# The upper halves of the attention one-hots made by ScalarE between its table copies

## The chip, the cores and the metric

The kernel runs on one core of one Trainium2 chip, as one launch. The metric is the device time of the launch in microseconds; the median of three runs of the kernel before is 3207.38 us (3206.33 to 3209.21). TensorE does the matrix products (PE in the rows, PEld for its weight loads), VectorE is DVE, ScalarE is ACT, GpSimd is POOL and SyncE, which issues most DMAs, is SP.

## The reference

Four graph layers run one after the other on 3750 nodes with 256 features, each on the layer-normalised, relu'd input, each added to it. The graph has 63750 edges, sorted by destination, with a type of 8 each. The change touches the first layer, a graph attention with one weight per edge type:

```python
feat_all = jnp.einsum('ni,rhid->rnhd', inputs, conv_weights)
feat_src_e = feat_all[edge_type, edge_src]
feat_dst_e = feat_all[edge_type, edge_dst]
el = jnp.sum(feat_src_e * attn_l[edge_type], axis=-1)
er = jnp.sum(feat_dst_e * attn_r[edge_type], axis=-1)
e = jax.nn.leaky_relu(el + er, negative_slope=LEAKY_SLOPE)
m = jax.ops.segment_max(e, edge_dst, num_segments=N_NODES)
ex = jnp.exp(e - m[edge_dst])
denom = jax.ops.segment_sum(ex, edge_dst, num_segments=N_NODES)
alpha = ex / denom[edge_dst]
h = jax.ops.segment_sum(alpha[..., None] * feat_src_e, edge_dst, num_segments=N_NODES)
```

The three layers behind it (a graph convolution, a network with edge features and a mean aggregation) are left as they are.

## The kernel before

Nodes lie in 30 tiles of 128, edges in 500 tiles of 128 that are gathered, weighted and summed by one-hot products. Each engine has its own program, written out in order; semaphores with the names below tie them together. Ahead of the loop over the edge tiles stands a prologue with three jobs that run side by side:

- **The table.** For each of the 30 node tiles TensorE computes the features of all 8 types in four parts (`table_part`, L871), two products of 128x512 each, into the PSUM banks 4 to 7 in turn. ScalarE copies each part (L599), before the four of a tile the attention terms of the sources (L595), and then writes the tile to HBM as `feat_d` (L603). A part waits for the copy of the part four before it (`tab_free`).
- **The attention term of the destinations, er.** For the 500 edge tiles, 50 iterations of ten, in two halves of five. SyncE loads the edges' places, counted from a node tile's start, into every partition (`RB`, from `rel_d`, L339). VectorE compares them with 0 to 127 (L1410, "low") and 128 to 255 (L1411, "high"), since five neighbouring edge tiles can reach over two node tiles; `OHT` holds both. TensorE multiplies them with er per node (`er_half`, L881 for low, L882 for high). VectorE reduces the result (L1430), multiplies it with the edge types (L1437) and sums it (L1440). At the start of each iteration TensorE's sequencer loads ten offsets into registers (L894).
- **Counts of equal edges.** VectorE counts them for four tiles an iteration (L1417) and writes them as bf16 (L1424, `val_ready`); GpSimd scatters them into the adjacency matrix `a_d` in HBM (L523). The first 200 tiles are done in the prologue.

On TensorE a half is put behind the table part at which its share of the 120 parts is reached: 100 halves to 120 parts. VectorE's order in an iteration is reduction of a half, both one-hots of the same half of the iteration after it, the same for the second half, product, sum, counts. The one-hots' buffer has one place for each half (0 and 1), so a half's one-hots wait for TensorE's half two before. Behind the loop GpSimd waits for its scatters, for VectorE and for all of `feat_d` in HBM, and gathers the 500 edge tiles (L532) among the remaining scatters.

Of the kernel before, what the change touches and what calls it, by code (L numbers as in the profile page):

```python
# [17 lines left out]
ALU = mybir.AluOpType  # L18
ACT = mybir.ActivationFunctionType
# [27 lines left out]
def gnn(nc, x, src, dst, edge_attr, edge_type, conv_w, attn_l, attn_r, h_bias, gcn_w, gcn_b, cluster,  # L47
# [10 lines left out]
    NT = -(-N // P)  # L58
# [5 lines left out]
    IT = T // 10  # L64
# [24 lines left out]
    with ExitStack() as ctx:  # L89
# [22 lines left out]
        IOTP = sb("IOTP", [P, 2])  # L112
# [42 lines left out]
        OHT = HSF[:, 4000:5280].bitcast(BF16).rearrange("p (h q e) -> p h q e", h=2, q=2)  # L155
# [33 lines left out]
        RB = [v.bitcast(BF16).rearrange("p (h e) -> p h e", h=2) for v in (SA[:, 6144:6784], SA[:, 7296:7936])]  # L189
# [67 lines left out]
        def s(name):  # L257
            if name not in S:
                S[name] = sem(name)
            return S[name]  # L260
# [36 lines left out]
        def mine(eng, ins, name, value):  # L297

            ins.then_inc(s(name), 1)
            eng.wait_ge(s(name), value)  # L300
# [16 lines left out]
        def counted_at(n):  # L317
# [3 lines left out]
            new = (k + 1) * CB // NB > k * CB // NB  # L321
            return c if new and c < T else None

        def ring(t):

            return SL[:, t % 10, :]
# [10 lines left out]
        def _(sp):  # L337
            def load(dst_ap, src_ap, name):
                sp.dma_start(dst_ap, src_ap).then_inc(s(name), 16)  # L339
# [6 lines left out]
            for a, t in ((dst, DI), (src, SI), (edge_type, TI)):  # L346
                v = t.rearrange("t (b e) -> t b e", b=LB)
                load(v[:, 0:LB - 1, :], a[0:(LB - 1) * LT * P].rearrange("(b t e) -> t b e", b=LB - 1, e=P), "edges_in")
                n = EFULL - (LB - 1) * LT
# [40 lines left out]
            with sp.Fori(0, IT // 2) as w:  # L390
                for b in range(2):
                    u = 2 * w + b
                    for h in range(2):
                        sp.wait_ge(s("oht_ready"), 2 * u + h + 1)
                        load(RB[b][:, h, :], rel_d[bass.ds((10 * u + 5 * h) * P, 5 * P)].partition_broadcast(P),
                             f"rows{b}_in{h}")
                    sp.wait_ge(s("val_ready"), u + 1)
                    load(KEYR[:, b, :, :].rearrange("p k n -> p (k n)"),
                         key_d[bass.ds(CT * u * P, CT * P)].partition_broadcast(P), f"rows{b}_in1")
# [167 lines left out]
        def _(act):  # L567
# [19 lines left out]
            act.wait_ge(s("small_in"), 16 * 15)  # L587
            act.activation(B1C, B1C, ACT.Relu).then_inc(s("b1_relu"), 1)

            act.wait_ge(s("elr_done"), 2 * 4)  # L590
            for t in range(NT):
                i = t % 2
                if t >= 2:
                    act.wait_ge(s(f"stage_out{i}"), 16 * (t // 2))
                act.activation(STAGE[:, i, :, D:RW], ELS[:, t, :].rearrange("p (r h) -> p r h", r=R),  # L595
                               ACT.Copy).then_inc(s("tab_el"), 1)
                for q in range(4):
                    act.wait_ge(s("tab_ps"), 4 * t + q + 1)
                    act.activation(STAGE[:, i, 2 * q:2 * q + 2, 0:D], PS[:, 4 + q, :].rearrange("p (r n) -> p r n", r=2),  # L599
                                   ACT.Copy).then_inc(s("tab_free"), 1)  # L600
                act.wait_ge(s("tab_free"), 4 * t + 8)
                act.wait_ge(s("tab_el"), t + 1)
                act.dma_start(rows(feat_d, t), STAGE[:, i, :, :].rearrange("p r n -> p (r n)")).then_inc(s(f"stage_out{i}"), 16)  # L603

            for i in range(2):
                act.wait_ge(s(f"stage_out{i}"), 16 * NJ)
            act.wait_ge(s("cont_ready"), 1)
# [212 lines left out]
        def _(pe):  # L820
# [53 lines left out]

            def er_half(u, h, qs):
                pe.wait_ge(s("oht_ready"), 2 * u + h + 5)
                pe.wait_ge(s("er_done"), 2 * u + h + 1)
                for k in range(5):
                    o = PS[:, h, k * 3 * RH:(k + 1) * 3 * RH]
                    q = qs[5 * h + k]  # L880
                    pe.matmul(o, OHT[:, h, 0, k * P:(k + 1) * P], ERB[:, bass.ds(q, 3 * RH)], start=True, stop=False)  # L881
                    last = pe.matmul(o, OHT[:, h, 1, k * P:(k + 1) * P], ERB[:, bass.ds(q + 3 * RH, 3 * RH)],  # L882
                                     start=False, stop=True)
                last.then_inc(s("er_ps"), 1)
# [3 lines left out]
            halves = 0  # L888
            for n in range(4 * NT):
                table_part(n // 4, n % 4)  # L890
                if halves * 4 * NT <= n * 2 * IT:
                    u, h = halves // 2, halves % 2
                    if h == 0:
                        _, qs = nc.values_load_multi_w_load_instructions(  # L894
                            QR[:, 10 * u:10 * u + 10], engines=[PE], min_val=0, max_val=(NT - 1) * 3 * RH,
                            skip_runtime_bounds_check_because="clamped to the last node tile when it was computed")
                    er_half(u, h, qs)
                    halves += 1
# [373 lines left out]
        def _(dve):  # L1272
# [134 lines left out]
            def dst_one_hot(u, h, b, v):  # L1407

                dve.wait_ge(s(f"rows{b}_in{h}"), 16 * (1 + h) * (v + 1))
                ts(OHT[:, h, 0, :], RB[b][:, h, :], IOTP[:, 0:1], None, ALU.is_equal)  # L1410
                mine(dve, ts(OHT[:, h, 1, :], RB[b][:, h, :], IOTP[:, 1:2], None, ALU.is_equal), "oht_ready", 2 * u + h + 5)  # L1411

            def counts(u, b):

# [537 lines left out]
```

## Time and profile before

| | |
|---|---|
| median of the runs | 3207.38 us |
| profiled execution, whole time | 3211.49 us |
| profiled execution, span of the program | 3209.7 us |
| TensorE busy | 2858.9 us (89%) |
| VectorE busy | 1866.8 us (58%) |
| ScalarE busy | 1257.0 us (39%) |
| GpSimd busy | 1017.9 us (32%) |
| first table part | 118.92 us |
| first gather of edge tiles | 478.57 us |

Times in the rows are microseconds from the span's start, unless marked ns. A timeline row gives the start, the duration, the engine, the line, the operation and, in brackets, the time that the engine stood idle before it and what ended that. The name there is the latest of the instructions that set a semaphore for it.

### The profile page before, as it was taken

The page shows a single profiled execution, that of the slowest core. Times are in us where ns is not written, and L with a number is a line of the kernel's source. Part 1 is how long each engine was busy: PE and PEld are TensorE (multiplying, and loading weights), DVE is VectorE, ACT ScalarE, POOL GpSimd, SP SyncE. Part 2 cuts the span into 40 slices and gives each one's busy share as a digit, 9 for nine tenths or more (in the row PEclk, how much of TensorE's full clock was granted, in tenths as well). Part 3 has the DMA queues.
Part 4 walks back from the last instruction along what each step waited for, and adds up shares of the span by engine and source line. Part 5 has one row for each costly group of instructions (what it writes and reads, how often), then busy time and mean ns, then how long its engine had stood idle before and what let it go on. Part 6 is the DMA issues. An engine that isn't in the chain of part 4 may idle for free.

```text
span 3209.7 us, 48246 instructions
## 1 busy us (share of the span) xinstructions
PE 2858.9 (89%) x15034; PEld 1892.2 (59%) x15034; DVE 1866.8 (58%) x5317; ACT 1257.0 (39%) x3665; POOL 1017.9 (32%) x1048
## 2 busy tenths in 40 slices
PE   1789885999999989897788999799999999999998
PEld 1544444999899888887144444455555555545446
DVE  6578884888878766667235433355555555513334
ACT  1122225787778777774004000144444444401000
POOL 3065567777777777776000000000000000000000
PEclk6599986999999999996968999899999999999999
DMA  8966654333333333321843333300000000132232
GB/s 237 402 187 183 194 173 112 101 91 89 89 86 88 89 86 87 88 55 34 299 146 118 102 102 100 106 7 3 7 5 5 7 3 7 38 102 70 83 102 78
DMA packets 245030, 317.60 MB, mean 99 GB/s; under 512 B 121467, under 2 KB 162084, under 8 KB 240740
## 3 DMA queue, kind: packets, MB, share of 16 engines
q1 hardware_dynamic: 191412, 179.07, 19.7%
q0 software_dynamic: 49104, 104.11, 10.9%
q10 hardware_dynamic: 4320, 31.95, 2.5%
q8 instruction: 108, 1.77, 0.2%
q14 instruction: 86, 0.70, 0.1%
HBM read 237.42 MB, written 77.59 MB: 98 GB/s over the span
## 4 chain that ended last, share of the span: by engine, by line
PE 49%; DVE 23%; issue 9%; ACT 5%; POOL 5%; DMA 5%; DVEq 4%; SPq 0%; POOLq 0%
PE PS L1153 17%; PE PS L998 15%; DVE SUMS L1567 4%; DMA BG<-a_d 3%; PE PS L822 3%; PE PS L939 3%; POOL BG L532 3%; PE PS L964 3%; PE PS L977 3%; POOL a_d L523 2%; ACT BG L653 2%; DVE BG L1703 2%; DVEq L1582 2%; DVE OHB L1430 2%; DVE X L1573 1%
## 5 line engine op out<-in xcount | busy, mean ns | idle before, releaser
L523 POOL DMA_INDIRECT a_d<-VAL,IDXS x499 | 492.4, 987 | 241.4 <-issue 135.9
L1153 PE MATMUL PS<-BG,SL 128*128 128x512 f32 (+1 forms) x1440 | 534.7, 527 | 12.2 <-ACT SL L736 12.2
L532 POOL DMA_INDIRECT BG<-feat_d,IDXST x500 | 490.4, 981 | 152.5 <-issue 127.2
L653 ACT ACTIVATE BG<-BG,SL 128x64 f32<-128x64 f32 x2000 | 513.5, 337 | 0.0
L1567 DVE TENSOR_TENSOR SUMS<-SUMS,PS 128x640 f32 x500 | 409.0, 818 | 165.6 <-PE PS L939 153.4
L1153 PEld LDWEIGHTS PS<-BG,SL 128*128 128x128 f32 x1440 | 273.9, 193 | 250.6 <-issue 222.4
L564 POOL MEMSET BG<- 128x7680 f32 x1 | 6.5, 6499 | 1297.1 <-DVE MV L1834 1297.1
L939 PE MATMUL PS<-OHB,BG 128*128 128x128 f32 x2000 | 339.2, 293 | 0.0
L977 PE MATMUL PS<-OHB,X 128*128 128x128 f32 x2000 | 319.5, 283 | 1.7 <-DVEq L1545 1.7
L977 PEld LDWEIGHTS PS<-OHB,X 128*128 128x128 f32 x2000 | 289.7, 197 | 14.7 <-issue 1.7
L964 PE MATMUL PS<-W1A,X 65*128 65x256 f32 x1000 | 276.0, 399 | 3.9 <-ACT X L627 0.9
L939 PEld LDWEIGHTS PS<-OHB,BG 128*128 128x128 f32 x2000 | 271.0, 197 | 0.6
L871 PE MATMUL PS<-SUMS,BG 128*128 128x512 f32 x480 | 244.1, 640 | 0.0
L723 ACT ACTIVATE SM<-SM,EPSC 128x1 f32<-128x1 f32 x60 | 17.7, 295 | 543.4 <-DVE SM L1795 543.4
L634 ACT ACTIVATE X<-PS 128x512 f32<-128x512 f32 x250 | 148.9, 596 | 154.9 <-PE PS L964 154.3
L822 PE MATMUL PS<-IDENT,X 128*128 128x128 f32 (+3 forms) x650 | 148.3, 274 | 65.9 <-DVE X L1486 26.8
L998 PE MATMUL PS<-AL,BG 128*128 128x512 bf16 (+1 forms) x924 | 193.2, 368 | 4.0 <-ACT BG L702 2.6
L998 PE MATMUL PS<-AL,SUMS 128*128 128x512 bf16 (+1 forms) x912 | 189.0, 364 | 3.9 <-DVE X L1906 2.8
L964 PEld LDWEIGHTS PS<-W1A,X 65*128 65x128 f32 x1000 | 175.4, 195 | 28.7 <-ACT X L627 8.5
L736 ACT ACTIVATE SL<-PS,COL 128x128 f32<-128x128 f32 x480 | 174.1, 476 | 26.0 <-PE PS L822 25.9
L599 ACT ACTIVATE SUMS<-PS 128x512 f32<-128x512 f32 x120 | 71.7, 597 | 272.5 <-PE PS L871 272.5
L1703 DVE TENSOR_TENSOR SUMS<-SUMS,OHB 128x2 f32 x499 | 81.6, 164 | 159.5 <-issue 93.5
(298 smaller groups left out, 4084.2 us busy)
## 6 DMA issues: line engine op xcount, KB each, us to landing
BG<-a_d SPq DMA_DIRECT2D x171, 256.0 KB, 4.2
AL<-a_d SPq DMA_DIRECT2D x137, 256.0 KB, 2.6
a_d<-BG POOLq DMA_DIRECT2D x30, 1088.0 KB, 40.4
feat_d<-SUMS ACTq DMA_DIRECT2D x30, 1040.0 KB, 5.0
BG<-rel_d SPq DMA_DIRECT2D x100, 160.0 KB
X<-in_edge_attr_dram SPq DMA_DIRECT2D x124, 128.0 KB
SUMS<-a_d SPq DMA_DIRECT2D x52, 256.0 KB, 2.6
SL<-key_d SPq DMA_DIRECT2D x50, 256.0 KB
```

The costliest lines, as they stand in the source:

```text
L523: pool.indirect_dma_start(a_d.rearrange("n (w o) -> (n w) o", o=1), bass.IndirectOffsetOnAxis(ap=IDXS[:, t:t + 1], axis=0), VAL[:, t:t + 1 ...
L532: pool.indirect_dma_start(RING[:, t // NB % 3, t % NB, :], None, feat_d.rearrange("n (r d) -> (n r) d", r=R), bass.IndirectOffsetOnAxis(ap ...
L653: last = act.activation(m, m, ACT.Copy, scale=EXT[:, b % 2, k, 1 + q:2 + q])
L736: last = act.activation(H1T[:, i, c, :], PS[:, 4 + 2 * i + c // 4, (c % 4) * P:(c % 4 + 1) * P], ACT.Relu, scale=COL8[:, 2 * l, c:c + 1], ...
L822: return pe.transpose(out_ap, in_ap, IDENT[0:k, 0:k])
L871: last = pe.matmul(PS[:, 4 + q, :], HT[:, c, t * P:(t + 1) * P], WALL[:, c, q * 512:(q + 1) * 512], start=(c == 0), stop=(c == 1))
L939: last = pe.matmul(at[:, (c + 1) * P:(c + 2) * P], RING[:, b % 3, k, c * P:(c + 1) * P], OH[:, k % 10, :], start=True, stop=True)
L964: last = pe.matmul(EDGE_HIDDEN[:, k * D:(k + 1) * D], EAT[v % 2][:, 2 * q + k, :], W1A[:, :], start=True, stop=True)
L977: pe.matmul(SUM_AT[n % 3][:, (3 + c) * P:(4 + c) * P], HM[v % 2][:, k, c * P:(c + 1) * P], OH[:, n % 10, :], start=True, stop=True)
L998: last = pe.matmul(PS[:, 4 * (g % 2) + 2 * c + o // 512, 0:m], lhs(t, part)[:, c * P:(c + 1) * P], rhs[:, o:o + m], start=(t == 0 and part ...
L1153: last = pe.matmul(PS[:, to + q, 0:width], lhs[:, i, c, :], w[:, c, q * width:(q + 1) * width], start=(c == 0), stop=(c == kc - 1))
L1567: add = tt(a, a, SUM_AT[n % 3].rearrange("p (a n) -> p a n", a=5), ALU.add)
```

## The change

The high one-hot leaves VectorE. ScalarE makes it with two operations: the absolute difference of the edges' places and 128 to 255, and the relu of one minus that, which is 1 where the difference is 0 and 0 elsewhere. Two pairs stand ahead of the table's copies; then, after the copy of a part behind which TensorE has a half, the pair for the half that comes two later. A new semaphore `oht_high` tells of it: TensorE waits for it before a half and SyncE before it loads a row buffer again. The rule by which halves stand among the parts is written as a function that both engines use; it gives TensorE the same order as before.

```diff
+        def halves_before(n):
+            return min(2 * IT, (n - 1) * 2 * IT // (4 * NT) + 1) if n else 0
...
                         sp.wait_ge(s("oht_ready"), 2 * u + h + 1)
+                        sp.wait_ge(s("oht_high"), 2 * u + h + 1)
                         load(RB[b][:, h, :], rel_d[bass.ds((10 * u + 5 * h) * P, 5 * P)].partition_broadcast(P),
...
+            def high_one_hot(u, h):
+                b, v = u % 2, u // 2
+                act.wait_ge(s(f"rows{b}_in{h}"), 16 * (1 + h) * (v + 1))
+                if u >= 1:
+                    act.wait_ge(s("er_ps"), 2 * (u - 1) + h + 1)
+                step(act.activation(OHT[:, h, 1, :], RB[b][:, h, :], ACT.Abs, bias=IOTP[:, 1:2], scale=-1.0))
+                act.activation(OHT[:, h, 1, :], OHT[:, h, 1, :], ACT.Relu, bias=1.0, scale=-1.0).then_inc(s("oht_high"), 1)
+
+            act.sem_inc(s("oht_high"), 4)
+            for h in range(2):
+                high_one_hot(0, h)
+            highs = 2
             act.wait_ge(s("elr_done"), 2 * 4)
...
+                    if highs < 2 * IT and halves_before(4 * t + q + 1) > highs - 2:
+                        high_one_hot(highs // 2, highs % 2)
+                        highs += 1
...
                 pe.wait_ge(s("oht_ready"), 2 * u + h + 5)
+                pe.wait_ge(s("oht_high"), 2 * u + h + 5)
...
-                if halves * 4 * NT <= n * 2 * IT:
+                if halves < halves_before(n + 1):
...
-                ts(OHT[:, h, 0, :], RB[b][:, h, :], IOTP[:, 0:1], None, ALU.is_equal)
-                mine(dve, ts(OHT[:, h, 1, :], RB[b][:, h, :], IOTP[:, 1:2], None, ALU.is_equal), "oht_ready", 2 * u + h + 5)
+                mine(dve, ts(OHT[:, h, 0, :], RB[b][:, h, :], IOTP[:, 0:1], None, ALU.is_equal), "oht_ready", 2 * u + h + 5)
```

ScalarE at the start of the table, before (the tile SUMS holds several buffers by name, the staging of the table among them; BG holds the row buffers; x20 is a count):

```order
L578 ACTIVATE SL<-X,NBI,RS 128x256 [waits n0_tp] x20
L588 ACTIVATE COL<-COL 128x2 [waits small_in]
L595 ACTIVATE SUMS<-SUMS 128x8x4 [waits elr_done]
L599 ACTIVATE SUMS<-PS 128x2x256 [waits tab_ps] x4
L603 DMA feat_d<-SUMS 128x2080 [waits tab_el,tab_free]
```

The same place after:

```order
L593 ACTIVATE COL<-COL 128x2 [waits small_in]
L601 ACTIVATE SUMS<-BG,IOTP 128x640 [waits rows0_in0]
L602 ACTIVATE SUMS<-SUMS 128x640 [waits act_steps]
L601 ACTIVATE SUMS<-BG,IOTP 128x640 [waits rows0_in1]
L602 ACTIVATE SUMS<-SUMS 128x640 [waits act_steps]
L613 ACTIVATE SUMS<-SUMS 128x8x4 [waits elr_done]
L617 ACTIVATE SUMS<-PS 128x2x256 [waits tab_ps]
L601 ACTIVATE SUMS<-BG,IOTP 128x640 [waits er_ps,rows1_in0]
L602 ACTIVATE SUMS<-SUMS 128x640 [waits act_steps]
L617 ACTIVATE SUMS<-PS 128x2x256 [waits tab_ps] x2
```

The absolute differences (L601) and relus (L602) now stand between the copies (L617), two pairs of them ahead of the first, and a copy waits behind the rows and the half that its pair waits for.

VectorE at the start of an iteration in its loop, before:

```order
L1430 TENSOR_REDUCE OHB<-PS 128x160 [waits er_ps]
L300 REGISTER_ALU
L1409 ISA [waits er_done]
L1410 TENSOR_SCALAR SUMS<-BG,IOTP 128x640 [waits rows1_in0]
L1411 TENSOR_SCALAR SUMS<-BG,IOTP 128x640
L300 ISA
L1429 REGISTER_ALU [waits oht_ready]
```

The same place after:

```order
L1452 TENSOR_REDUCE OHB<-PS 128x160 [waits er_ps]
L300 REGISTER_ALU
L1432 ISA [waits er_done]
L1433 TENSOR_SCALAR SUMS<-BG,IOTP 128x640 [waits rows1_in0]
L300 ISA
L1451 REGISTER_ALU [waits oht_ready]
```

One of the two one-hots is gone; every wait of VectorE stands as before.

## Rows read from the trace of the kernel before

**Rows 1.** Sums by engine: stretch, length, busy (count); granted clock, DMA share, GB/s.

```profile
169.30:472.88 303.58, 276.81 (x1364) 138.89 (x1365) 243.78 (x782) 71.89 (x137) 179.60 (x185) 0.96 0.62 183
```

**Rows 2.** Groups of instructions, 169.3 to 472.88: count | busy, mean ns | idle before.

```profile
L599 ACT ACTIVATE SUMS<-PS 128x512 f32<-128x512 f32 x110 | 65.7, 597 | 224.8 <-PE PS L871 224.8
...
L1410 DVE TENSOR_SCALAR SUMS<-BG,IOTP 128x640 bf16<-128x640 bf16 x92 | 40.9, 445 | 12.4
L1411 DVE TENSOR_SCALAR SUMS<-BG,IOTP 128x640 bf16<-128x640 bf16 x92 | 34.8, 378 | 0.0
...
L595 ACT ACTIVATE SUMS<-SUMS 128x32 f32<-128x32 f32 x27 | 6.2, 229 | 11.3 <-ACT SUMS L599 11.3
```

**Rows 3.** Timeline of one iteration, 302 to 306 us, VectorE and one half.

```profile
303.69 0.37 DVE L1411 TENSOR_SCALAR SUMS<-BG,IOTP 128x640 bf16<-128x640 bf16 x1
...
304.20 0.21 PE L881 MATMUL PS<-BG,SUMS 128*128 x1 [1.17 <-DVE SUMS L1411]
...
304.97 0.39 DVE L1410 TENSOR_SCALAR SUMS<-BG,IOTP 128x640 bf16<-128x640 bf16 x1
...
305.28 0.38 DVE L1411 TENSOR_SCALAR SUMS<-BG,IOTP 128x640 bf16<-128x640 bf16 x1
...
305.84 0.49 DVE L1437 TENSOR_TENSOR OHB<-OHB,SUMS 128x320 f32<-128x320 f32 x1 [0.19 <-DVE SUMS L1411]
```

**Rows 4.** Waits in 169.3 to 472.88: engine and releaser, total us, times, longest.

```profile
PE PS L881 <- DVE SUMS L1411: 24.6, 21, 1.8
PE PS L881 <- DVE OHB L1430: 1.7, 2, 1.1
...
DVE OHB L1430 <- PE PS L882: 8.7, 4, 5.1
```

**Rows 5.** TensorE's register loads, ns min/median/max: all 50, and that near 307.

```profile
L894 PEldq TENSOR_LOAD <-BG x50: 1072/2412/10539, 117.0 to 466.2; - x50
...
L894 PEldq TENSOR_LOAD <-BG x1: 3911/3911/3911, 307.1 to 307.1; - x1
```

**Rows 6.** Timeline of TensorE, 307 to 318 us.

```profile
307.19 0.21 PE L881 MATMUL PS<-BG,SUMS 128*128 x1
...
307.61 1.95 PE L871 MATMUL PS<-SUMS,BG 128*128 128x512 f32 x4
311.25 0.21 PE L881 MATMUL PS<-BG,SUMS 128*128 x1 [1.69 <-DVE SUMS L1411]
...
312.52 5.00 PE L871 MATMUL PS<-SUMS,BG 128*128 128x512 f32 x8
```

**Rows 7.** ScalarE's groups by form over the whole span: count | busy, mean ns.

```profile
L653 ACT ACTIVATE BG<-BG,SL 128x64 f32<-128x64 f32 x2000 | 513.5, 337 | 0.0
...
L765 ACT ACTIVATE SUMS<-SL 128x512 f32 x39 | 25.0, 641 | 23.7 <-DVE SL L1857 12.6 <-DVE SL L1851 11.1
...
L702 ACT ACTIVATE BG<-SL 128x1280 bf16<-128x1280 f32 x6 | 7.6, 1270 | 0.2
```

**Rows 8.** Timeline of the start: first copy, second low one-hot, a late half.

```profile
122.74 0.60 ACT L599 ACTIVATE SUMS<-PS 128x512 f32<-128x512 f32 x1 [11.93 <-PE PS L871]
...
134.90 0.39 DVE L1410 TENSOR_SCALAR SUMS<-BG,IOTP 128x640 bf16<-128x640 bf16 x1 [2.61 <-DMA SL<-key_d]
...
148.05 0.26 PE L881 MATMUL PS<-BG,SUMS 128*128 x1 [6.49 <-issue]
```

**Rows 9.** Timeline of the prologue's end: last values, scatter, table write, first gather.

```profile
472.81 0.17 DVE L1424 CAST VAL<-BG 128x4 bf16<-128x4 f32 x1
...
473.25 0.95 POOL L523 DMA_INDIRECT a_d<-VAL,IDXS  x1 [0.84 <-DVE VAL L1424]
...
473.73 0.33 ACTq L603 DMA_DIRECT2D feat_d<-SUMS  x1
...
478.57 0.99 POOL L532 DMA_INDIRECT BG<-feat_d,IDXST  x1 [0.44 <-issue]
...
508.33 0.29 DVE L1484 TENSOR_TENSOR X<-BG,AL 128x80 f32<-128x80 f32 x1 [19.37 <-DMA BG<-feat_d,IDXST]
```

More of the change, by code:

```diff
@@ L603, in _ @@
                 act.dma_start(rows(feat_d, t), STAGE[:, i, :, :].rearrange("p r n -> p (r n)")).then_inc(s(f"stage_out{i}"), 16)
+            assert highs == 2 * IT
             for i in range(2):
```

## Prediction
> **What bounds the kernel now.** I first looked where the two engines that the change touches work together: the prologue, in which TensorE alternates table parts with halves of the attention term, VectorE makes the one-hots and counts, and ScalarE only copies. I took it as the stretch from 169.30 us (the reduction of iteration 3, after the DMA crowd of the start) to 472.88 us (that of iteration 49): 46 iterations in 303.58 us, 6.60 us each. In the sums by engine [rows 1] TensorE is busy 276.81 us, VectorE 243.78, ScalarE 71.89. A share of 80% does not make VectorE look like the limit, so the next view is the order of its work [rows 3]: reduction of a half, one-hot low, one-hot high, the same for the second half, product, sum, counts. Between these operations stand only short gaps in which it waits for its own result (0.19 us before the product at 305.84). The waits say the same [rows 4]: VectorE waited 8.7 us for TensorE in the whole stretch, four times, one of them 5.1 us at its very beginning. VectorE therefore sets the pace, by a chain of its own work.
>
> TensorE is close behind. It waited 24.6 us for the one-hots by the profile [rows 4]. That is too much, because a second thing holds the first half of an iteration: TensorE's sequencer loads ten offsets from SBUF into registers, 1.07 to 10.54 us, median 2.41 [rows 5]. The half at 311.25 is put down to the one-hot, but the load that began at 307.1 took 3.91 us and ended at 311.0 [rows 5, 6]. The half at 304.20 is a true wait for VectorE: the one-hot high of that half ended at 304.06 [rows 3]. A half released that late takes 1.27 us to the next table part (311.25 to 312.52), and one that was ready 0.42 us (307.19 to 307.61) [rows 6].
>
> **VectorE loses one operation per half.** The first one-hot runs from 304.97 to 305.36, the second, which starts before the first is done, from 305.28 to 305.66 [rows 3]; without it the chain goes on from 305.36. That is 0.30 us per half, not the 0.378 us of the operation [rows 2], because the two overlap. With 92 halves in the stretch it makes 27.6 us; VectorE alone would then need 276.0 us, 6.00 us per iteration. The iterations before 169.30 us I count at nothing: there the register load holds TensorE, 6.49 us before the half at 148.05 [rows 8], and a shorter VectorE chain only waits longer.
>
> **ScalarE gains 200 operations.** No row shows this shape; the nearest ones are 128x512 in 641 ns and 128x1280 in 1270 ns, both SBUF to SBUF [rows 7]. The line through them gives 0.82 ns a column and 746 ns for 640. The first of the pair has a bias by partition; a 128x64 with one such operand takes 337 ns [rows 7], 63 above that line, so 0.81 us. The relu follows only when the absolute difference is written. The bounds of that wait are 0 and 0.42 us (11.3 us in 27 waits of ScalarE for itself, each with a DMA issue in it [rows 2]); I take 0.1, since the issue fills most of the 0.42. The pair costs 1.66 us (1.56 to 1.98). An iteration has two pairs, 110/46 = 2.4 copies of 0.597 us [rows 2] and 0.6 of the 0.23 us copies with their 0.42 us wait: 3.3 + 1.4 + 0.4 = 5.1 us (4.9 to 5.8), under the 6.0 us of VectorE. ScalarE idles 224.8 us for table parts in the stretch [rows 2]; 92 pairs take 153 us of it. Price of the position: a pair stands ahead of the next copy, and waits for the half two before its own. TensorE has four banks for parts, so a copy that is one pair (1.7 us) late holds nothing, and the pair has two halves and two parts of time before it is needed (2 x (0.42 + 1.95) us, of which the pair takes 1.7) [rows 6]. I put it at zero; without this cover each iteration would pay up to 1.7 us. The Trainium skill speaks against the change: "ScalarE: Activation LUTs", Rules for kernel authors, wants relu and the like on VectorE, up to about three times faster per element in bf16. The trace agrees on the operation (0.378 us against my 1.66). The same page, What ACT_TABLE_LOAD costs, would price the pair at 719 + 812 = 1.53 us, an estimate by its formula, and the iteration at 4.9 us.
>
> **Waits that are added.** SyncE waits for the high one-hot too before it refills a row buffer; queued behind are the other row loads and the key loads. The high half needs only TensorE's half two before it, the low one VectorE's reduction of that half too, so the new wait is met first: zero (if it came last, a row load would go out later by up to the 1.7 us of a pair, and it has an iteration of time). At the start two pairs stand ahead of all table copies, and the second needs the rows and keys on which VectorE waited until 134.90 us; the first copy goes from 122.74 to about 137 us [rows 8]. Four free banks hide it: part 4 is the first that needs a bank back, and it stands behind the half at 148.05 us. Uncovered it would cost 14 us. TensorE checks one more semaphore per half: between 0 and 0.14 us, which is all that passes from the end of a one-hot to the half that it releases (304.06 to 304.20) [rows 3]. While TensorE is not the limit this is zero; if it were, 92 halves would pay at most 13 us.
>
> **What is late next.** TensorE. Its stretch without true waits lies between two bounds. If half of the 26.3 us of waits [rows 4] was the register load and everything else stays, it needs 303.6 - 13 = 290 us. If all waits go, and with them the 0.85 us by which each of the 23 late halves was slow, it needs 303.6 - 26.3 - 19.6 = 258 us. Some table parts also run slow after such a wait: two took 5.00 us at 312.52 instead of 1.95 each [rows 6], at a mean granted clock of 0.96 of the 2.4 GHz level in the stretch [rows 1]. The result is the later of 276 (VectorE) and 258 to 290 (TensorE), with some waiting of each for the other. I take the middle of 276 and 290, 283 us: a gain of 20.6. At the end the table's last write is issued at 473.73 and the first gather starts at 478.57, right after the last four scatters, which follow from the values written at 472.81 [rows 9]. If TensorE now trails VectorE, that write comes later by part of a microsecond: -0.6. From the gather the chain runs on (VectorE waits 19.37 us for the first twenty, until 508.33), so the prologue's gain moves all behind it.
>
> Sum: 3211.49 - 20.6 + 0.6 = 3191.5 us in the profiled execution, which lies 4.1 above the median of 3207.38; as a median 3187.4 us.
>
> **The rivals.**
> - TensorE keeps the pace. The register load gets longer when the row and key loads come closer together, and holds the first half of each iteration. For it: 3.91 us at 307.1 against a minimum of 1.07, and 10.54 when the DMA queues were full [rows 5]. Against it: in half of the waits VectorE was last. The stretch is 290 to 300 us; gain 3 to 13, 3194 to 3204.
> - The wait only changes its name, or a later stage gives the gain back. Halves would wait for the high one-hot instead of the low, if a pair took about 2.3 us (two pairs 4.6, with 1.8 of copies 6.4). Nothing before 508 us is tied to a fixed time, which speaks against the second form. 3201 to 3213.
> - ScalarE takes over and it is slower. This is the page's rule as a mechanism of this kernel: work goes to the engine that is slower at it. The place is the pair between two copies, and it decides from (6.60 - 1.8)/2 = 2.4 us per pair. At 2.7 us an iteration takes 7.2, 0.6 more than now, 28 us in 46: 3235 us. The rows of 641 and 1270 ns [rows 7] speak against it.
>
> **How the numbers follow.** Forecast (stretch 276 to 290, 3179 to 3194): 0.64. TensorE keeps the pace: 0.15. No change: 0.10. ScalarE: 0.07. More than VectorE's 27.6 us (slow table parts vanish too): 0.04. This measurement can tell about 0.2%, 6.4 us, from no change, so faster means below 3201. Faster: 0.64 + 0.11 + 0.04 = 0.79. Same: 0.04 + 0.10 = 0.14. Slower: 0.07. The range reaches from a little beyond VectorE's whole gain, 3178, to the end of the first rival, 3203.
>
> **What would show it.** In the changed kernel VectorE's iteration should be 6.0 to 6.3 us, its waits for TensorE's halves should grow from the 8.7 us, and TensorE's waits for the low one-hot should fall below 24.6. The pair on ScalarE should take 1.6 to 2.0 us and no half should wait for the high one-hot. The first gather should start at 455 to 465 us instead of 478.57. I am wrong if the pair is above 2.3 us, if register loads of 4 us become common, or if the first gather comes earlier and the end does not.

## The result and the profile after

The changed kernel takes 3187.25 us (median of 5 runs, 3185.04 to 3194.47) against 3208.3 us (5 runs) for the kernel before beside it: a ratio of 0.9933 with a 95% interval of 0.9914 to 0.9951. That is 21 us faster, at the predicted time of 3187.4. The profiled execution took 3186.24 us, its span 3184.4 us. The nearness to the predicted median hides that some terms were off and cancelled, so the trace is read first.

The same stretch, reduction of iteration 3 to that of iteration 49, now runs from 170.85 to 449.33 us. Its sums by engine in the changed kernel (stretch, length; busy us and count of PE, PEld, DVE, ACT, POOL; granted clock, DMA share, GB/s) answer to [rows 1]:

```profile
170.85:449.33 278.48, 264.04 (x1362) 133.46 (x1363) 217.00 (x690) 206.56 (x321) 174.25 (x182) 0.98 0.67 199
```

The stretch went from 303.57 to 278.48 us, 6.60 to 6.05 per iteration. VectorE has 92 instructions fewer and is busy 26.8 us less, 0.29 per half; ScalarE has 184 more and 134.7 us more.

The groups by form of the stretch (count | busy, mean ns of one | idle before, releasers) answer to [rows 2]:

```profile
L601 ACT ACTIVATE SUMS<-BG,IOTP 128x640 bf16<-128x640 bf16 x92 | 75.7, 822 | 42.8 <-PE PS L905 41.5 <-DMA SL<-key_d 1.3
L602 ACT ACTIVATE SUMS<-SUMS 128x640 bf16<-128x640 bf16 x92 | 67.8, 737 | 2.9
L617 ACT ACTIVATE SUMS<-PS 128x512 f32<-128x512 f32 x110 | 65.6, 597 | 28.6 <-PE PS L893 20.1
...
L1433 DVE TENSOR_SCALAR SUMS<-BG,IOTP 128x640 bf16<-128x640 bf16 x92 | 41.0, 446 | 12.4
```

The pair is 0.822 + 0.737 us and a gap of 0.03, 1.59 us. ScalarE idled 224.8 us for table parts before; now it still idles 42.8 and 28.6 us, in front of pairs and copies. One low one-hot costs VectorE what it did (446 ns against 445).

The timeline of VectorE in one iteration (start, length, engine, line, operation) answers to [rows 3]. L1452 is the reduction, L1433 the low one-hot, L1459 the product:

```profile
304.96 0.66 DVE L1452 TENSOR_REDUCE OHB<-PS 128x160 f32<-128x480 f32 x1
...
305.76 0.62 DVE L1433 TENSOR_SCALAR SUMS<-BG,IOTP 128x640 bf16<-128x640 bf16 x1
...
306.51 0.66 DVE L1452 TENSOR_REDUCE OHB<-PS 128x160 f32<-128x480 f32 x1
...
307.29 0.39 DVE L1433 TENSOR_SCALAR SUMS<-BG,IOTP 128x640 bf16<-128x640 bf16 x1
...
307.87 0.49 DVE L1459 TENSOR_TENSOR OHB<-OHB,SUMS 128x320 f32<-128x320 f32 x1 [0.19 <-DVE SUMS L1433]
```

The product waits for the one remaining one-hot by the same 0.19 us by which it waited for the second one before. VectorE's chain is still without a long gap, one link shorter.

The waits of the stretch (releaser: total us, times, longest) answer to [rows 4]:

```profile
PE PS L904 <- DVE SUMS L1433: 10.1, 13, 1.8
PE PS L904 <- DVE OHB L1452: 3.4, 3, 1.5
PE PS L904 <- issue: 0.6, 2, 0.3
...
DVE OHB L1452 <- PE PS L905: 11.8, 8, 6.2
```

TensorE's waits for VectorE fell from 26.3 to 13.5 us. Of VectorE's 11.8 us, 6.2 stand ahead of the very first reduction, as 5.1 of the 8.7 did before; inside the stretch it waits 5.6 us for TensorE, 3.6 before. None of the halves in the stretch waits for ScalarE.

These rows name the semaphore that came last and never a register load. So the ends of the loads (L894 before, L917 after) and of the one-hots were compared half by half in the two traces: a wait is the load's where the load ended after the one-hot. Before, 10.2 us (7 halves) were the load's and 16.2 us (16 halves) the one-hot's; after, 9.7 us (9 halves) are the load's and 4.5 us (9 halves) the one-hot's. The waits for the one-hot fell, those for the loads stayed.

At the prologue's end the timeline (with what ended an engine's idle time in brackets) answers to [rows 9]:

```profile
449.25 0.17 DVE L1446 CAST VAL<-BG 128x4 bf16<-128x4 f32 x1
...
449.70 0.96 POOL L528 DMA_INDIRECT a_d<-VAL,IDXS  x1 [0.86 <-DVE VAL L1446]
...
451.08 0.33 ACTq L624 DMA_DIRECT2D feat_d<-SUMS  x1
...
455.84 0.99 POOL L537 DMA_INDIRECT BG<-feat_d,IDXST  x1 [1.40 <-DMA feat_d<-SUMS]
...
485.61 0.29 DVE L1506 TENSOR_TENSOR X<-BG,AL 128x80 f32<-128x80 f32 x1 [19.38 <-DMA BG<-feat_d,IDXST]
```

The first gather starts 22.73 us earlier (455.84 against 478.57), and VectorE's wait for the first twenty gathers is 19.38 us against 19.37. The account: 25.1 gained in the stretch, 1.54 lost ahead of it, 0.82 lost behind it, where the first gather now waits for the table's last write, and idles 1.40 us instead of 0.44. From the gather to the end it is 2728.6 us against 2731.1.

### The profile page after: what moved, and what is told of

Same layout as the page of the kernel before. It is cut to its first block, busy times and chain, and to the rows that moved or that the text cites. A ratio compares the mean times of both kernels' runs of the same rounds, so it can differ in the third digit from the quotient of the medians.

```text
span 3184.4 us, 48481 instructions
## 1 busy us (share of the span) xinstructions
PE 2844.6 (89%) x14970; PEld 1887.5 (59%) x15034; DVE 1838.6 (58%) x5217; ACT 1403.1 (44%) x3865; POOL 1015.7 (32%) x1048
## 4 chain that ended last, share of the span: by engine, by line
PE 51%; DVE 23%; issue 8%; ACT 6%; DMA 5%; POOL 4%; DVEq 4%; SPq 0%; POOLq 0%
PE PS L1176 17%; PE PS L1021 15%; DVE SUMS L1589 4%; DMA BG<-a_d 3%; PE PS L987 3%; PE PS L844 3%; PE PS L962 3%; PE PS L1000 3%; ACT BG L675 3%; DVE BG L1725 2%; POOL BG L537 2%; DVEq L1604 2%; POOL a_d L528 2%; DVE OHB L1452 2%; DVE X L1595 2%
## 5 line engine op out<-in xcount | busy, mean ns | idle before, releaser
L528 POOL DMA_INDIRECT a_d<-VAL,IDXS x499 | 488.8, 980 | 219.4 <-issue 134.7
L987 PE MATMUL PS<-W1A,X 65*128 65x256 f32 x1000 | 276.0, 399 | 3.9 <-ACT X L649 0.9
L745 ACT ACTIVATE SM<-SM,EPSC 128x1 f32<-128x1 f32 x60 | 17.7, 295 | 540.7 <-DVE SM L1817 540.7
L893 PE MATMUL PS<-SUMS,BG 128*128 128x512 f32 x480 | 240.0, 631 | 0.0
L1725 DVE TENSOR_TENSOR BG<-BG,OHB 128x2 f32 x499 | 81.9, 164 | 144.7 <-issue 85.8
```

The costliest lines, as they stand in the source:

```text
L528: pool.indirect_dma_start(a_d.rearrange("n (w o) -> (n w) o", o=1), bass.IndirectOffsetOnAxis(ap=IDXS[:, t:t + 1], axis=0), VAL[:, t:t + 1 ...
L893: last = pe.matmul(PS[:, 4 + q, :], HT[:, c, t * P:(t + 1) * P], WALL[:, c, q * 512:(q + 1) * 512], start=(c == 0), stop=(c == 1))
L987: last = pe.matmul(EDGE_HIDDEN[:, k * D:(k + 1) * D], EAT[v % 2][:, 2 * q + k, :], W1A[:, :], start=True, stop=True)
L1725: step(tt(a, a, held[:, :, n:n + 1], ALU.add))
```

## The experiments

**The theory:** VectorE's chain set the pace, so the operation taken from it is the whole gain, and ScalarE's pair is hidden by the two halves of lead with which it is issued. **The rivals:** the pair has a price somewhere; TensorE, with its register loads, sets the pace after the change. The part behind the first gather varies between 2725 and 2744 us from one profiled execution to another, so the stretch, reduction 3 to reduction 49, is the sharper measure. Each stretch is that of one profiled execution; two kernels whose stretches should be equal differ by 0.2 us (before and e1) and 1.8 us (after and e2). All ratios are to the kernel before, run beside.

| kernel | stretch us | first gather us | median us | ratio, 95% interval |
|---|---|---|---|---|
| before | 303.57 | 478.57 | 3208.3 | 1 |
| after | 278.48 | 455.84 | 3187.25 | 0.9933, 0.9914 to 0.9951 |
| e1, operation back on VectorE | 303.35 | 479.31 | 3207.42 | 1.000, 0.9991 to 1.001 |
| e2, before without the high one-hot | 280.29 | 455.97 | 3191.53 | 0.9947, 0.9931 to 0.9964 |
| e3, half an operation more on ScalarE | 283.90 | 461.44 | 3192.19 | 0.9949, 0.9933 to 0.9966 |
| e4, a whole one more | 288.26 | 466.11 | 3198.41 | 0.9972, 0.9963 to 0.9982 |
| e5, after with one register load | 275.10 | 439.39 | 3172.48 | 0.9876, 0.9855 to 0.9897 |
| e8, before with one register load | 302.54 | 467.52 | 3195.61 | 0.9963, 0.9949 to 0.9977 |
| e6, pair one half ahead | 323.42 | 500.84 | 3234.06 | 1.0074, 1.0058 to 1.0089 |
| e11, e6 with one register load | 275.29 | 441.13 | 3176.93 | 0.99, 0.9881 to 0.9918 |
| e7, after, a load of 20 every second iteration | 273.17 | 449.81 | 3172.63 | 0.9884, 0.9867 to 0.9902 |
| e9, before, the same loads of 20 | 301.13 | 465.57 | 3200.35 | 0.9968, 0.9959 to 0.9978 |
| e10, after, loads of 30 | 316.01 | 493.05 | 3225.02 | 1.0044, 1.0028 to 1.0059 |

### e1 and e2: is it VectorE's operation?

e1 keeps ScalarE's pair and gives VectorE its second one-hot again, written to a place that nobody reads:

```diff
+        SCR = OHB[:, 840:1160].bitcast(BF16)
...
-                mine(dve, ts(OHT[:, h, 0, :], RB[b][:, h, :], IOTP[:, 0:1], None, ALU.is_equal), "oht_ready", 2 * u + h + 5)
+                ts(OHT[:, h, 0, :], RB[b][:, h, :], IOTP[:, 0:1], None, ALU.is_equal)
+                mine(dve, ts(SCR, RB[b][:, h, :], IOTP[:, 1:2], None, ALU.is_equal), "oht_ready", 2 * u + h + 5)
```

> The changed kernel, with VectorE making its second one-hot again, into a place that nobody reads; ScalarE, the waits and TensorE stay as changed. Theory (the gain is VectorE's shorter chain and nothing else): the 46 iterations from the reduction of iteration 3 to that of iteration 49 take 303 us again instead of 278.5, and the time is back at 3208, between 3204 and 3213. Rival (the gain comes from elsewhere, the waits or the released upper half): it stays near 3187.

e2 is the kernel before without the high one-hot: nothing in its place, on either engine; the upper halves are set to zero once, ahead of the loop.

```diff
+            step(dve.memset(OHT[:, :, 1, :], 0.0))
...
-                ts(OHT[:, h, 0, :], RB[b][:, h, :], IOTP[:, 0:1], None, ALU.is_equal)
-                mine(dve, ts(OHT[:, h, 1, :], RB[b][:, h, :], IOTP[:, 1:2], None, ALU.is_equal), "oht_ready", 2 * u + h + 5)
+                mine(dve, ts(OHT[:, h, 0, :], RB[b][:, h, :], IOTP[:, 0:1], None, ALU.is_equal), "oht_ready", 2 * u + h + 5)
```

> The kernel before without the high one-hot: it is zero all through, so the part of er that lies in a second node tile is left out; ScalarE does only its copies. Theory (ScalarE's 200 operations and their waits cost nothing): as the changed kernel, 3187 within 4 us, stretch 276 to 280 us. Rival (the pairs hold something that the profile does not show): 3180 or less.

The sums by engine of the stretch, e1 first, then e2 (columns as above):

```profile
170.04:473.39 303.35, 276.82 (x1364) 138.74 (x1365) 244.23 (x782) 207.93 (x321) 176.52 (x183) 0.96 0.59 183
```

```profile
169.13:449.42 280.29, 266.37 (x1362) 133.95 (x1363) 216.90 (x690) 72.00 (x137) 176.26 (x184) 0.97 0.64 198
```

e1 has the ScalarE of the changed kernel (207.93 us) and the VectorE of the kernel before (244.23 us), and the stretch of the kernel before, to 0.2 us. e2 has the VectorE of the changed kernel and the ScalarE of the kernel before, and the changed kernel's stretch within 1.8 us. So the whole gain is VectorE's operation. ScalarE's pair costs nothing that can be seen: without it the stretch is no shorter.

### e3 and e4: what a pair may cost

Both add a copy of the one-hot onto itself behind the relu, of 320 columns (e3) and of 640 (e4), so that the pair becomes longer and its result later. The edit of e4:

```diff
-                act.activation(OHT[:, h, 1, :], OHT[:, h, 1, :], ACT.Relu, bias=1.0, scale=-1.0).then_inc(s("oht_high"), 1)
+                step(act.activation(OHT[:, h, 1, :], OHT[:, h, 1, :], ACT.Relu, bias=1.0, scale=-1.0))
+                act.activation(OHT[:, h, 1, 0:640], OHT[:, h, 1, 0:640], ACT.Copy).then_inc(s("oht_high"), 1)
```

> The changed kernel with a third ScalarE operation in each pair, a copy of 320 columns onto itself: the pair goes from 1.59 to about 2.07 us, ScalarE's iteration from 5.0 to about 5.9 us, just under the 6.05 of the changed kernel. Theory (ScalarE has an iteration's remainder as its slack): 3187 to 3192. Rival (ScalarE is already near its limit, because it waits in order for TensorE): 46 x 0.96 us slower, up to 3231.

> As the run before, but with all 640 columns copied: the pair takes about 2.36 us, ScalarE's iteration about 6.5 us. Theory (ScalarE then sets the pace): the stretch grows by 46 x 0.45 = 21 us to about 300 us, 3208, so that the whole gain is gone. Rival (the two halves of lead hide it): 3187 to 3192.

ScalarE's groups in the stretch of e4 (L601, L603 and L618 are the absolute difference, the added copy and the table copy):

```profile
L601 ACT ACTIVATE SUMS<-BG,IOTP 128x640 bf16<-128x640 bf16 x92 | 75.4, 820 | 18.1 <-PE PS L906 18.0
...
L603 ACT ACTIVATE SUMS<-SUMS 128x640 bf16<-128x640 bf16 x92 | 67.8, 737 | 2.9
...
L618 ACT ACTIVATE SUMS<-PS 128x512 f32<-128x512 f32 x110 | 63.6, 582 | 4.1 <-PE PS L894 3.9
```

In e4 a pair takes 2.36 us, ScalarE is busy 262.0 of 288.3 us and idles 26 us, 0.6 in an iteration of 6.27; half of the stretch's gain is still there in time (288.3 lies 15.3 below 303.6 and 9.8 above 278.5). In e3 a pair takes about 2.07 us and the stretch is 5.4 us longer than the changed kernel's, though the intervals of the whole times overlap. The price in the stretch thus begins between 1.6 and 2.1 us a pair, before ScalarE is full. In e4 VectorE waits 22.2 us for TensorE's halves, in the changed kernel 11.8; without the waits ahead of the first reduction that is 17.7 against 5.6, which covers the 9.8. TensorE's waits for halves there, 23 us before 19 halves, were each ended by a register load that finished after the pair's result: a late pair seems to push back the next load, as is shown for e6 below. e3 came out at the edge of what was expected (3187 to 3192), e4 between its two expectations. By the working of the prediction's third rival, an iteration with e4's pair takes 2 x 2.36 + 1.8 = 6.5 us, hardly less than before; it takes 6.27. That working thus puts the end of the gain too early, and it says nothing of its beginning to shrink: at 2.36 us 10 of the 25 us are gone.

### e6 and e11: what the lead of two halves is worth

e6 issues each pair one half ahead of its use instead of two:

```diff
-                    if highs < 2 * IT and halves_before(4 * t + q + 1) > highs - 2:
+                    if highs < 2 * IT and halves_before(4 * t + q + 1) > highs - 1:
```

> The changed kernel with each pair on ScalarE one half later, so that it is made one half before it is needed instead of two. Theory (the lead of two halves is the cover of the pair): a ready half comes 0.42 + 1.95 us after the half before it, copy and pair take 0.6 + 1.6 us behind the part, so the pair is ready at about the moment of need; halves wait for the high one-hot now and then, TensorE trails, stretch 279 to 290 us, 3187 to 3199. Rival (the lead is not needed): stretch 278.5 within 1 us, 3187. Rival (a late pair holds every half): 300 us or more.

The stretch grew to 323.42 us, 44.9 more than the changed kernel's, and the kernel is slower than before the change. From the timelines of e6, first the relu of one half on ScalarE, then TensorE's halves (L904) and table parts (L893):

```profile
279.31 0.74 ACT L602 ACTIVATE SUMS<-SUMS 128x640 bf16<-128x640 bf16 x1
```

```profile
280.24 0.21 PE L904 MATMUL PS<-BG,SUMS 128*128 x1
...
281.55 1.95 PE L893 MATMUL PS<-SUMS,BG 128*128 128x512 f32 x4
284.26 0.21 PE L904 MATMUL PS<-BG,SUMS 128*128 x1 [0.77 <-issue]
...
285.52 1.95 PE L893 MATMUL PS<-SUMS,BG 128*128 128x512 f32 x4
287.30 0.21 PE L904 MATMUL PS<-BG,SUMS 128*128 x1
```

TensorE idled only 0.1 us before the half at 280.24: the relu had ended at 280.05, while a table part was still running. But the half took 1.31 us to the next part (281.55), where one that had been released long before takes 0.42 (307.56 to 307.98 in the changed kernel). The expectation (279 to 290 us) failed, and no row of these halves shows a long wait for the relu. The rows of TensorE's sequencer in e6 tell what lies between its products, and what comes after the half (count: ns min/median/max, first and last start):

```profile
L904 PEldq FUSED_REGOPS  x500: 46/46/46, 132.7 to 494.9; - x167
```

```profile
L917 PEldq TENSOR_LOAD <-BG x1: 2413/2413/2413, 281.5 to 281.5; - x1
```

Each product of a half has an address operation of 46 ns on the sequencer (500 on L904, as many on L905). In these timelines the operations of a half start 124 ns apart, with one longer step, and the two halves differ in when they start. First those of the low products in the changed kernel's half at 307.56, then those in e6's half at 280.24:

```profile
L904 PEldq FUSED_REGOPS  x5: 46/46/46, 306.4 to 307.4; - x5
```

```profile
L904 PEldq FUSED_REGOPS  x5: 46/46/46, 280.1 to 281.3; - x5
```

In the changed kernel they began 1.1 us ahead of the half, while TensorE worked off a table part, and its products then started 42 ns apart. In e6 the first began at 280.14, behind the relu's end at 280.05, and the products came 124 ns apart, at the pace of the operations. The register load of the next iteration starts only behind the late half, at 281.5, takes 2.41 us, and the next half at 284.26 comes late and slow again (1.26 us). Counting the halves of the last 47 iterations whose ten products take over 0.7 us gives 54 of 94 in e6, 41 before, 29 in the changed kernel. Against the changed kernel e6's halves take about 20 us more in the stretch. Register loads that end after the relu and the one-hot hold 19 halves for 27.7 us, 18 us more, and the table parts take 6 us more, at a granted clock of 0.96 instead of 0.98. These are sums over TensorE's work in the two traces; the waits for the one-hot, which fell, go against them.

If that is the reason, the lead is worth nothing once loads and address operations are gone. e11 is e6 with the load of iteration 0 for all iterations, which also takes the address operations away:

```diff
-                    if h == 0:
+                    if h == 0 and u == 0:
```

> Pairs one half later and one register load for all iterations (er from the wrong node tiles), in which TensorE also has no address operations between the products of a half after the first iteration. Theory (the pairs one half later cost 45 us because a half that is released late takes 1.25 instead of 0.42 us, its address operations not being done ahead): without them the stretch is 276 to 285 us, 3172 to 3182. Rival (the late pair holds TensorE by itself): the stretch stays above 300 us, 3215 or more.

Sequencer and stretch of e11:

```profile
L904 PEldq FUSED_REGOPS  x10: 46/46/46, 132.9 to 138.3; - x10
```

```profile
160.18:435.47 275.29, 242.39 (x1359) 116.20 (x1357) 216.08 (x692) 202.11 (x319) 183.09 (x192) 1.00 0.71 211
```

With the pair issued as late as in e6, the stretch is 275.29 us; all of the loss is gone. So the price of a short lead is not the wait itself but what the wait keeps TensorE's sequencer from doing. Loads and address operations went together here; no run at this lead takes away only one of them, and e6's sums above put the two at about the same.

### e5, e8, e7, e9 and e10: the register loads

e5 is the changed kernel and e8 the kernel before, both with the line of e11's diff.

> The changed kernel with one register load instead of 50: TensorE uses the ten offsets of iteration 0 in all iterations, so er is taken from the wrong node tiles. Theory (VectorE sets the pace also after the change, TensorE's loads only lengthen it a little, from 6.00 to 6.05 us): the stretch from iteration 3 to 49 goes from 278.5 to 276 us, and the two late halves of the start (loads of 10 us) go, some 8 to 10 us: 3176. Rival (TensorE with its loads now sets the pace): the stretch falls to 265 us or less, 3165 or less.

> The kernel before with one register load instead of 50, the offsets of iteration 0 throughout, er from the wrong node tiles. Theory (VectorE alone set the pace): the stretch from iteration 3 to 49 stays at 301 to 303 us, and only the start gains 8 to 10 us: 3199. Rival (the loads shared in the pace already): stretch below 298 us.

The waits of the stretch in e5, to be held against those of the changed kernel:

```profile
PE PS L904 <- DVE SUMS L1433: 32.3, 27, 1.4
...
DVE SUMS L1433 <- DMA SL<-key_d: 3.2, 2, 1.7
DVE OHB L1452 <- PE PS L905: 0.7, 3, 0.2
```

```profile
311.12 0.22 PE L904 MATMUL PS<-BG,SUMS 128*128 x1 [1.22 <-DVE SUMS L1433]
...
311.56 1.95 PE L893 MATMUL PS<-SUMS,BG 128*128 128x512 f32 x4
```

In e5 VectorE waits 0.7 us for TensorE and TensorE 32.3 us for the low one-hot: VectorE sets the pace. The 275.1 us are not its chain alone, since it waits 3.2 us for key loads, which it does not do in the changed kernel; e7 below, where it waits for neither, takes 273.2. A half that is released late is as fast as any, 0.44 us (311.12 to 311.56). In e8 the stretch is 302.54 us, 1.0 less than before, with 2.3 us of waits for keys in it; before, VectorE had waited 3.6 us for TensorE inside the stretch. **Before the change loads and address operations had little share in the pace**, at most 3.6 of 303.6 us, and more in the start, where the reduction of iteration 3 comes at 159.45 us instead of 169.31.

e7 keeps all offsets but loads 20 at a time, in every second iteration; e9 does that to the kernel before, and e10 loads 30 at a time.

```diff
-                    if h == 0:
+                    if h == 0 and u % 2 == 0:
...
-                            QR[:, 10 * u:10 * u + 10], engines=[PE], ...
+                            QR[:, 10 * u:10 * u + 20], engines=[PE], ...
...
-                    er_half(u, h, qs)
+                    er_half(u, h, qs[10 * (u % 2):])
```

> The changed kernel with one register load of 20 offsets for two iterations instead of one of ten for each, 25 instead of 50. Theory (a load costs mostly by itself and not by its count): iteration 1 finds its offsets loaded, one of the two 10 us stalls of the start goes, 5 us, and the stretch falls by 1 to 2 us: 3181. Rival (a load costs by the offset): the loads take twice as long, the stretch grows, 3187 or more.

> The kernel before with one register load of 20 offsets for two iterations. Theory (VectorE alone paced the kernel before, TensorE's loads only its start): stretch 302 to 303 us, one of the two late halves of the start goes: 3200 to 3204. Rival (fewer loads help whatever paces): 3195 or less, as much as they brought to the changed kernel.

> The changed kernel with one register load of 30 offsets for three iterations, 17 in all. Theory (VectorE paces at 5.95 us with few loads as with one): stretch 272 to 276 us as with 25 loads, the start 5 us earlier than with them since iterations 1 and 2 find their offsets loaded: 3165 to 3173. Rival (a long load holds TensorE as much as two short ones): 3175 or more.

TensorE's register loads in the changed kernel (the answer to [rows 5]), in e7 and in e10:

```profile
L917 PEldq TENSOR_LOAD <-BG x50: 1074/2410/10357, 117.7 to 443.6; - x50
```

```profile
L917 PEldq TENSOR_LOAD <-BG x25: 1356/1387/5027, 129.6 to 432.0; - x25
```

```profile
L917 PEldq TENSOR_LOAD <-BG x17: 1364/7101/20322, 116.4 to 475.2; - x17
```

The sums of e7's stretch (columns as above):

```profile
170.97:444.14 273.17, 260.13 (x1360) 130.95 (x1358) 216.54 (x691) 206.27 (x322) 175.90 (x184) 1.00 0.68 208
```

Twenty offsets take a median of 1.39 us where ten take 2.41, and there are half as many. e7's stretch is 273.2 us, 5.3 below the changed kernel's, more than the 1 to 2 expected: the 5.6 us for which VectorE waited there are gone, and its waits show none for TensorE and none for keys. So 273.2 us is VectorE's own chain. The address operations are all still there, with 27 slow halves against 29, so slow halves alone do not hold VectorE; the loads do. e7's median 3172.63 is the fastest of all kernels here that compute the whole: 14.6 us under the changed kernel. In its profiled execution (3189.3 us) the first load began 12 us later than in the others, at 129.6, so the first gather at 449.81 shows less of the gain than the median does. In e9 the same edit gives 2.4 us in the stretch and about 10 ahead of it, and 9.6 us (0.32%) in all. So most of e7's 14.6 us could have been had before the change too; about 5 are new. Loads of 30 have a median of 7.1 us. TensorE waits for 39.4 us before 7 halves, each behind a load that ends 0.3 us earlier, and e10 is slower than before the change, as its rival had it. Why 30 are so much slower than 20 stays open.

## Why the prediction was right, and where it was not

The bound and the mechanism held: VectorE's chain set the pace, and one link less is the gain. The time held too, its closeness by luck. Point by point:

- **The operation removed: right.** 0.30 us per half was read from starts that overlap, instead of the operation's 0.378; VectorE's busy time fell by 0.29 per half. Its chain alone was put at 276.0 us; where nothing else holds it, it takes 273.2 (e7). The 276.0 still held the 3.6 us for which VectorE had waited inside the stretch; 303.6 - 3.6 - 27.6 gives 272.4.
- **What is late next: mis-sized.** I took 283 us, the middle between VectorE's 276 and a TensorE bound of 290; it was 278.5, a gain of 25.1 instead of 20.6. That half of TensorE's waits were register loads and would stay was not far off: 10.2 of 26.3 us, and 9.7 afterwards. The step that failed is "everything else stays" in the 290. TensorE's time in the halves fell by 6.8 us, with 29 slow halves instead of 41, and that in the table parts by 4.4 us, at a granted clock of 0.98 instead of 0.96. The 278.5 are VectorE's chain of 273.2 (e7) and the 5.6 us for which it waits inside the stretch, to 0.3 us. Taking the middle of two bounds came near it without that working.
- **A half released late is slow: right in size, wrong in cause.** The 0.85 us do not come with the late release by itself: e5's late half takes 0.44 us. They come with address operations that were not done ahead (e6's timelines). I counted 23 such halves, those with a wait; 41 of the last 94 were slow.
- **ScalarE's pair: right.** 1.59 us against 1.66 (1.56 to 1.98). By the formula of the Trainium skill ("ScalarE: Activation LUTs", What ACT_TABLE_LOAD costs) the two operations come to 812 and 719 ns, an estimate; the trace agrees, with 822 and 737. The Trainium skill ("ScalarE: Activation LUTs", Rules for kernel authors) wants relu on VectorE. For the operation the trace agrees, 1.59 us for the pair against 0.378. For the kernel it was the chain that counted: the pair took 0.30 us per half off VectorE's, and e2, where nobody does the work, is no faster.
- **The pair's position: zero was right, and the bound without cover was not passed.** I wrote up to 1.7 us per iteration; e6 took one half of the lead away and lost 44.9 us, 0.98 per iteration. Two halves and two parts do cover the pair, one of each does not; and the loss is the sequencer's (e11), which the prediction had not seen.
- **No half waits for the high one-hot: right in the stretch.** At the start one does: the timeline of the changed kernel has

```profile
133.10 0.26 PE L904 MATMUL PS<-BG,SUMS 128*128 x1 [9.66 <-ACT SUMS L602]
```

  The relu ended 0.17 us after the low one-hot there, and the half came 0.75 us after the low one-hot began (132.35); before, it came 0.81 after (131.62 to 132.43). It cost nothing.
- **The start: zero against 1.54 us.** Of these, 0.73 stand ahead of anything that the change touches: TensorE's product of ones, the last before the prologue, starts at 117.69 instead of 116.96. The reduction of iteration 0 is 0.68 late, and 0.86 more come between it and that of iteration 3, where the register loads take up to 10.4 us. Other kernels with the pair reach iteration 3 between 170.0 and 170.9 us, e2 without it at 169.13. Whether up to 0.9 us of it is a price of the pair is not settled.
- **The end: -0.6 against -0.82,** by the mechanism that was named (the table's last write is late).
- **From the gather the gain moves on: right.** 22.7 us there, 25.25 in the profiled execution, 21 in the medians. At the gather the sum had 20.0. The profiled execution was put at 3191.5 us and took 3186.24: 4.5 more gained in the stretch, 1.5 and 0.2 less at the start and the end, 2.5 gained behind the gather, which no term has. That the median came out at 3187.25 against 3187.4 is luck: the sum took 4.1 us off the profiled time to reach a median, and the changed kernel's profiled execution lies 1.0 below its median.

Of the rivals, "TensorE keeps the pace" (290 to 300 us) fell with 278.5; "the wait changes its name" with the waits above; "ScalarE takes over" did not come about at 1.59 us; longer pairs cost time (e3, e4), but in e4 TensorE's waits end with its register loads. A gain of more than 27.6 us did not come in the stretch (25.1). Register loads of 4 us and more did not become common: 4 of the last 46 before, 5 after.

## What to carry to other kernels

Work may go to an engine that does it four times slower if that engine idles and the other one's chain sets the pace; the first thing to read is which engine goes from one operation to the next without a long wait, not which has the highest busy share. Moved work needs a lead: put it where its result is there before the consumer's sequencer reaches the wait, because here a sequencer that waited did not prepare the work behind the wait. Once the longest chain is cut, look again at what cost little before: halving the number of register loads gave 2.4 us in the stretch before this change and 5.3 after it. And compare with the same edit on the kernel before: of the 14.6 us that it gave in all, 9.6 were there already.

## What had not been expected of the hardware

- A register load of 20 values has a lower median (1.39 us of 25) than one of 10 (2.41 us of 50), and one of 30 takes 7.1 us (of 17, up to 20.3). The shortest took 1.36, 1.07 and 1.36 us, so the count by itself does not order them. In the kernel before, the load at 254.5 took 4.03 us with a DMA share of 0.95, and that at 263.0 1.08 us with 0.00. Number, size and place of the loads changed together, and the cause stays open.
- A half of ten products takes 0.42 us when TensorE's sequencer was ahead of it and 1.25 to 1.31 when it was not; its products then follow the address operations, 124 ns apart instead of 42 (e6), and the difference is gone where the operations are gone (e5, e11).
- The granted clock of the stretch differs by kernel, as a share of the 2.4 GHz level: 0.92 in e10, 0.96 before and in e1, e3, e6 and e8, 0.98 after, 1.00 in e5, e7 and e11. It does not go by TensorE's waits alone: e5 with 34.5 us of them before halves has 1.00, the changed kernel with 14.1 has 0.98. How much of the gains is the clock's was not measured by itself.
